# Another order of the work behind the last projection, on TensorE, ScalarE and VectorE

## What is computed

```python
def _act_quant(x):
    scale = 127.0 / jnp.clip(jnp.max(jnp.abs(x), axis=-1, keepdims=True), 1e-05)
    return jnp.clip(jnp.round(x * scale), -128.0, 127.0) / scale
gate = jax.nn.silu(_bitlinear(x, w_gate))      # 256 -> 1024, ternary weights
up = _bitlinear(x, w_up)                       # 256 -> 1024
return _bitlinear(gate * up, w_down)           # 1024 -> 256
```

## Time and profile before

| | |
|---|---|
| time, median of 3 runs (lowest to highest) | 574.09 us (573.98 to 574.76) |
| the profiled execution: its own time | 573.64 us |
| the profiled execution: its span in the trace | 570.9 us |
| busy over the whole span | PE 91%, DVE 60%, ACT 50%, POOL 20% |
| the stretch that the change touches | 541 us to the end of the span |

### The profile page before, as it was taken

The page is one execution under the profiler, slowest core; times in us unless marked ns, Lnnn a source line. Parts: engine busy times, 40 slices in busy tenths (PEclk is TensorE's granted clock), DMA queues, the critical chain, the costliest instruction groups (busy, mean ns, idle before and its releaser), DMA issues.

```text
span 570.9 us, 15296 instructions
## 1 busy us (share of the span) xinstructions
PE 520.9 (91%) x6590; PEld 407.1 (71%) x6590; DVE 344.4 (60%) x658; ACT 287.9 (50%) x518; POOL 113.9 (20%) x130
## 2 busy tenths in 40 slices
PE   5888898999998989999998989999999989999854
PEld 2566665988777666988776758988667669997623
DVE  5978357567565555565653666574754475643586
ACT  1265754632445465534347446343565667527573
POOL 5241200012241100011423000020721000451110
PEclk9999999999999999999999999999999999999998
DMA  8400070020420020200501200201400200000001
GB/s 303 184 2 2 3 298 36 2 75 1 172 90 2 3 75 3 75 0 1 223 2 38 77 2 1 75 0 49 175 2 30 76 1 2 0 1 1 3 1 43
DMA packets 5516, 30.40 MB, mean 53 GB/s; under 512 B 1218, under 2 KB 2114, under 8 KB 3779
## 3 DMA queue, kind: packets, MB, share of 16 engines
q1 hardware_dynamic: 5442, 29.35, 13.8%
HBM read 28.82 MB, written 0.52 MB: 51 GB/s over the span
## 4 chain that ended last, share of the span: by engine, by line
PE 78%; DVE 10%; ACT 8%; issue 2%; DMA 0%; POOL 0%; DVEq 0%; ACTq 0%
PE psD L354 16%; PE QD L714 14%; PE psD L727 10%; PE QD L450 7%; PE QD L490 5%; DVE AQ L1986 4%; ACT PTR L1388 4%; PE psD L348 3%; PE psD L510 3%; PE QD L483 3%; PE psD L714 2%; PE psD L531 2%; PE psD L517 2%; PE psD L391 2%; DVE MX L1983 2%
## 5 line engine op out<-in xcount | busy, mean ns | idle before, releaser
L1388 ACT ACTIVATE PTR<-QD 128x2048 f32<-128x2048 f32 x40 | 75.1, 1878 | 52.9 <-PE QD L490 46.2
L1986 DVE TENSOR_REDUCE AQ<-QD 128x8 f32<-128x2048 f32 (+1 forms) x24 | 55.0, 2292 | 29.4 <-PE QD L450 29.3
L714 PE MATMUL QD<-HH,WFH 128*128 128x256 f32 x224 | 69.0, 308 | 0.0
L2734 POOL TENSOR_TENSOR rstd<-ms,mhalf 128x2 f32<-128x2 f32 x26 | 18.3, 702 | 232.6 <-ACT HE L1354 231.5
L714 PE MATMUL QD<-HL,WFH 128*128 128x256 f32 x224 | 63.3, 283 | 0.0
L714 PE MATMUL QD<-HH,WFL 128*128 128x256 f32 x224 | 63.3, 282 | 0.0
L1983 DVE TENSOR_REDUCE MX<-QD 128x16 f32<-128x2048 f32 x16 | 36.7, 2293 | 39.6 <-PE QD L450 39.6
L727 PE MATMUL psD<-WC,HID 128*128 128x256 f32 x256 | 58.5, 381 | 0.0
L2091 DVE TENSOR_TENSOR WFL<-WC,WFH 128x512 fp32r<-128x512 f32 x64 | 44.4, 700 | 18.6 <-ACT WFH L1434 18.1
L354 PE MATMUL psD<-WAB,hT 128*128 128x256 f32 (+1 forms) x152 | 53.1, 487 | 1.0 <-DVE hT L1924 1.0
L2781 POOL TENSOR_SCALAR_AFFINE_SELECT PTR<-PTR 128x1024 f32<-128x1024 f32 (+1 forms) x24 | 34.5, 1438 | 93.1 <-ACT PTR L1388 93.1
(11 more groups left out here) (211 smaller groups left out, 979.9 us busy)
## 6 DMA issues: line engine op xcount, KB each, us to landing
WC<-in_wc SPq DMA_DIRECT2D x4, 3072.0 KB, 10.3
WAB<-in_wb SPq DMA_DIRECT2D x4, 1024.0 KB, 4.8
WF<-in_wf SPq DMA_DIRECT2D x1, 3072.0 KB, 10.9
WAB<-in_wa SPq DMA_DIRECT2D x3, 1024.0 KB, 5.8
bias<-in_bias SPq DMA_DIRECT2D x3, 512.0 KB, 3.7
WAB<-in_wt SPq DMA_DIRECT2D x1, 1024.0 KB, 5.5
X<-in_x SPq DMA_DIRECT2D x2, 256.0 KB, 3.9
WAB<-in_wa SPq DMA_DIRECT2D x1, 512.0 KB, 5.0
```

What stands on the lines that cost most here:

```text
L714: mm = pe.matmul(S[:, w * L:(w + 1) * L], wp[:, m, :], hp[:, k, :], start=(k == 0 and j == 0), stop=(k == KT - 1 and j == 2))
L1388: nc.scalar.activation(PTR[:, r % 2, :], QD[:, :], ACT.Exp, scale=SCALE if r < SELF_ROUNDS else 1.0).then_inc(t_exp, 1)
L1986: v = dve.tensor_reduce(QKR[b][:, t, 0, h, MAXROW].rearrange("p (s r) -> p r s", r=SG_H), QD[:, :].rearrange("p (r s n) -> p r s n", r=4, ...
```

## The change

Six pieces of the hand-written order are put elsewhere; no instruction is added, removed or altered. On TensorE the first half of tile 3's gate and up goes ahead of `hidden_T(0)`, `quantised_down(0)` ahead of `hidden_T(1)`, and `quantised_down(1)` ahead of the last tile's transposes. On ScalarE `ternary(3)` goes to the front, and roundings go behind the next gates. On VectorE the scales of a tile move between the products of the next, `hidden_T(0)` and `output(0)` go ahead of `hidden_max(3)`, and `window_sum_gamma(1)` goes ahead of `rounded_T(0)`. The bank rotation becomes rounded_T 0, rounded_T 1, hidden_T 0, down 0, hidden_T 1, hidden_T 2, down 1, last 0, last 1, down 2, down 3.

```diff
--- before.py
+++ after.py
@@ -1251,15 +1251,15 @@
                 rounded_T(1)
                 quantised_gate_up(2, 0)
                 quantised_gate_up(2, 1)
+                quantised_gate_up(3, 0)
                 hidden_T(0)
-                quantised_gate_up(3, 0)
                 quantised_gate_up(3, 1)
+                quantised_down(0)
                 hidden_T(1)
-                quantised_down(0)
                 hidden_T(2)
+                quantised_down(1)
                 last_hidden_T(0)
                 last_hidden_T(1)
-                quantised_down(1)
                 quantised_down(2)
                 quantised_down(3)
 
@@ -1869,6 +1869,7 @@
                 ternary(2)
                 copy_oT(NL, 1, "pw1")
                 silu_table()
+                ternary(3)
                 quantised_gates(0, 0)
                 quantised_gates(0, 1)
                 centre(1)
@@ -1877,14 +1878,13 @@
                 unbias_tokens(1)
                 quantised_gates(1, 1)
                 scale_hidden(0)
-                unbias_hidden(0)
                 quantised_gates(2, 0)
                 quantised_gates(2, 1)
+                unbias_hidden(0)
+                quantised_gates(3, 0)
                 scale_hidden(1)
+                quantised_gates(3, 1)
                 unbias_hidden(1)
-                quantised_gates(3, 0)
-                quantised_gates(3, 1)
-                ternary(3)
                 scale_hidden(2)
                 unbias_hidden(2)
                 scale_last_hidden()
@@ -2669,8 +2669,8 @@
                 layernorm_apply(6, 0, X0, hs, done)
                 round_tokens(0)
                 window_sum_stats(1)
+                window_sum_gamma(1)
                 rounded_T(0)
-                window_sum_gamma(1)
                 window_residual(1)
                 layernorm_stats(7, 1, X0)
                 quantised_hidden(0, 0)
@@ -2679,32 +2679,32 @@
                 hidden_max(0)
                 quantised_hidden(1, 0)
                 hidden_clamp(0)
+                hidden_inverse(0)
                 rounded_T(1)
-                hidden_inverse(0)
                 quantised_hidden(1, 1)
                 hidden_max(1)
+                quantised_hidden(2, 0)
                 hidden_clamp(1)
+                quantised_hidden(2, 1)
                 hidden_inverse(1)
-                quantised_hidden(2, 0)
-                quantised_hidden(2, 1)
                 hidden_max(2)
+                hidden_T(0)
+                hidden_clamp(2)
                 quantised_hidden(3, 0)
-                hidden_clamp(2)
+                hidden_inverse(2)
                 quantised_hidden(3, 1)
-                hidden_inverse(2)
+                output(0)
                 hidden_max(3)
-                hidden_T(0)
                 hidden_clamp(3)
                 hidden_T(1)
                 hidden_inverse(3)
                 scale_last_hidden()
                 round_last_hidden(0)
-                output(0)
                 round_last_hidden(1)
                 hidden_T(2)
                 last_hidden_T(0)
+                output(1)
                 last_hidden_T(1)
-                output(1)
                 output(2)
                 output(3)
```

## The result

The changed kernel takes 572.68 us, median of 12 runs (571.71 to 574.13); the kernel before took 573.98 (12 runs, 573.63 to 574.82). The ratio is 0.9976, 95% interval 0.9969 to 0.9984: 1.3 us faster, where 2.6 were forecast. The time lies in the range and on the forecast side; the gain is half of the sum. The profiled execution has a span of 569.9 us and a time of 573.96. Two of the prediction's own signs of being wrong appeared in it: a granted clock of 0.50 behind 541, and VectorE standing still for 0.87 us at a product of tile 2.

A forecast was written before the change was run, and what follows sets the result against it. TensorE bounds the whole kernel, but the last stage is a loop through three engines with VectorE stalls. Removing waits sums to 2.55, rounded 2.6 us: profiled 573.64 to 571.0, median forecast 571.5, range 570.7 to 572.9.

The forecast's parts named there:

- the sum: Last stage: VectorE's end moves from 567.77 to 565.22, a gain of 2.55, rounded to 2.6 us.
- the prediction's own signs of being wrong: Clock of 0.50 behind 541, VectorE waiting for a gate, or last store over 3.1 us after the last output.
- The walk: Last stage's new order timed step by step on VectorE, ScalarE and TensorE: gate stalls gone, last output from 564.74.
- The three thin margins: Tile 2's second gate, tile 3's last gate and output(0) ready just before VectorE wants them; first two by 0.11, 0.08.
- the rival of the thin margins: VectorE waits for ScalarE again, products 0.3 to 0.4 us late, 1.2 us back: 572.7; chance 0.13.
- The front at 0: Moving ternary(3) and window_sum_gamma(1) forward costs 0, covered by VectorE's layer norm; ends: gain 0, loss 0.9 us.
- the slower rival: Longer idle before the first gate-up group drops TensorE's clock, never regained: 4.8 us lost, 576.3; chance 0.04.
- The clock: Rival: TensorE falls to half clock from about 560.6, between down groups, 1.1 to 1.2 us back: 572.7; chance 0.15.
- the forecast 568.3: Span from the profile expected if the prediction was right, with the last output near 564.7.
- the time outside the span: Difference between profiled time and span; not named, carried over unchanged in going from 573.64 to 571.0.
- two rivals at 572.7: Late clock fall, chance 0.15, and thin margins not holding, chance 0.13; both inside the range's upper end of 572.9.
- Stores: End of kernel: stores keep about 0.86 us spacing, and 3.1 us from last output's end to span end stay.

The follow-up runs named there:

- e3: Changed kernel with 8, 5 and 5 unread matmuls filling TensorE's idle before the first gate-up group, rounded_T(1) and hidden_T(2): 569.88 us, ratio to before 0.9922.
- e10: Changed kernel with the 8, 5 and 5 unread matmuls, and quantised_down(1) put back behind the last tile's transposes: 570.66 us, ratio to before 0.9940.
- e11: Changed kernel with the 8, 5 and 5 unread matmuls, and ScalarE's rounding of tile 0 back before tile 2's gates: 570.57 us, ratio to before 0.9934.
- e12: Changed kernel with window_sum_gamma(1) put back behind rounded_T(0) and 5, 5 and 5 unread matmuls in TensorE's idle: 569.78 us, ratio to before 0.9921.
- e4: Kernel before with 5, 5 and 12 unread matmuls in TensorE's idle, the 12 in front of the first down group: 572.46 us, ratio to before 0.9966.
- e9: Changed kernel with 12 matmuls added only in a program copy this input does not run: 570.76 us, ratio to before 0.9941.
- e5: Changed kernel with 12 unread matmuls behind the last down group: 571.04 us, ratio to before 0.9938.
- e6: Kernel before with 12 unread matmuls behind the last down group: 573.06 us, ratio to before 0.9973.
- e7: Changed kernel with 8 unread matmuls in front of the first gate-up group only: 571.07 us, ratio to before 0.9941.

## Why the prediction came out as it did

**The walk: right.** Every stall that was said to go is gone, and no new one came, once the clock is the one it was made for; the last output of e3 is 0.16 us off after 12.5 us of walk. The three thin margins (0.11, 0.08 and 0.14 us) held, with 0.08, 0.02 and 0.07 us left in e3 by the same handing-over times, so the rival of the thin margins did not occur. The pieces that were tried alone came to 0.8 and 0.7 us (e10, e11), 0.41 and 0.68 in the stage. In the changed kernel as it stands the walk does not hold: it falls behind at the first gate-up groups and at tile 2, by 1.51 us in all.

**The front at 0: right in its price, wrong in its safety.** VectorE's layer norm covers `window_sum_gamma(1)` (e12). But I had taken the clock as full in front of 558, and in the changed kernel's profile it fell at the first gate-up groups. The mechanism stood in the text only as the slower rival, priced as one that never gets the clock back; it does get it back.

**The clock: half right.** That it falls all the same was a rival, at 1.1 to 1.2 us and late, behind 560. It fell early and in the middle, 1.5 us in the profiled execution and 0.9 in the mean. Its lesson is the other side of the difference: I took the profiled execution of before as what before does, while its mean span is 571.6, 0.7 above the 570.9 of the profile. Both kernels lose some 0.9 to 1.2 us to falls (e4 sets only a lower bound for before), so the clock did not take the missing half. That the span shrank by just the sum is luck: the changed kernel's mean span came out 0.8 above the forecast 568.3 and before's 0.7 above its base, and the two errors cancel.

**The step that failed: the time outside the span was taken to stay, without a reason.** The prediction does not name it; in going from 573.64 to 571.0 it carried 573.64 - 570.9 = 2.74 us over unchanged. It was 2.79 in the mean of before and became 3.79. That term, 1.0 us too small, is what separates a gain of 2.5 from one of 1.5 in these means (1.3 in the medians). None of the rivals named it. What made it grow is shown as far as TensorE's program, whose lengthening takes it away (e9); the mechanism stays open. With the program of both lengthened (e5 against e6) the change is worth 571.04 - 573.06 = -2.0 us, all of it in the span, so the missing half is not this term alone in every pair of runs.

**The range: right by luck.** Its upper part was there for two rivals at 572.7, a late fall of the clock and thin margins. The measured 572.68 came about otherwise, by earlier falls in both kernels and by the time outside the span.

**Stores: right.** The last two outputs keep their spacing (they start at 565.78 and 566.66), and the span ends 2.8 us behind the last output's end, against 3.1.

## What to carry to other kernels

Here a new order could be costed to 0.16 us over 12.5 us from start to start distances in one trace, with every engine's queue and every handing over walked, for an execution without falls of the clock. Still, take the spans of several runs as the base, since one execution may have met fewer clock falls than the mean. In a stage where TensorE has little to do, unread matmuls kept its clock up at no cost where they fitted into its idle (e3), delayed the next group where they did not (e4), and one gap filled was not enough (e7). And measure a stage from a common step inside it, not by the span. Last, watch the time outside the span: if it changes while the span does what it should, try a longer program before you look for a cause in the work.

## What the runs showed that I had not expected

The time outside the span was 1.68 to 1.83 us in every run of the ten kernels with a longer TensorE program (one run of e6 had 1.88), and 1.83 to 4.37 in the four without, where it takes steps, most of about 0.3 us (1.85, 2.4, 2.7, 3.0, 3.2, 3.55, 3.8, 4.1, 4.4). Twelve matmuls that are never executed are worth 1.9 us in the changed kernel. Which block, branch or wait makes it so was not found, and whether a longer program of another engine does the same was not tried. Falls of the clock came after idles of 2.40 us and of 1.4 to 1.8 us between short groups; in the first profile such idles had left it at full.
